# Moving a row norm, its scale factors and a token product in the written order of a two-stream recurrence

## The reference, cut to what matters

```python
gate = ki @ w0_;  hb = ki @ w2_;  sg = silu(gate);  hidden = sg * hb
dhidden = vi @ w1_.transpose(0, 2, 1)
dhbm = dhidden * sg;  dgate = dhidden * hb;  dgba = silu_backprop(dgate, gate)
w1g = newtonschulz5(einsum(hidden * lr1i, vi))      # two steps:
w0g = newtonschulz5(einsum(ki * lr0i, dgba))        #   A = X X^T; Bm = b A + c A A
w2g = newtonschulz5(einsum(ki * lr2i, dhbm))        #   X = a X + Bm X
w1_ = w1_ + w1g                                     # same for w0_, w2_
w1_ = w1_ / (norm(w1_, axis=1) + 1e-05) * w1n       # same for w0_, w2_
oi = silu(qi @ w0_) * (qi @ w2_) @ w1_
```

## Time and profile before

| | |
|---|---|
| time, median of 3 runs | 1683.79 us (1683.41 to 1691.88) |
| span of the profiled execution | 1633.0 us (its own time is not given; the 50.8 us between span and median lie around the instructions) |
| PE busy | 1477.8 us, 90% |
| DVE busy | 1275.3 us, 78% |
| ACT busy | 1004.9 us, 62% |
| POOL busy | 788.0 us, 48% |
| granted PE clock in 300 to 750 us | 1.00 |

### The profile page before, as it was taken

The page is one execution under the profiler, slowest core; times in us unless marked ns, Lnnn a source line. Parts: engine busy times, 40 slices in busy tenths (PEclk is TensorE's granted clock), DMA queues, the critical chain, the costliest instruction groups (busy, mean ns, idle before and its releaser), DMA issues. The chain is left out here.

```text
span 1633.0 us, 44257 instructions
## 1 busy us (share of the span) xinstructions
PE 1477.8 (90%) x12478; PEld 987.5 (60%) x12543; DVE 1275.3 (78%) x4523; ACT 1004.9 (62%) x2284; POOL 788.0 (48%) x837
## 2 busy tenths in 40 slices
PE   7995899999999999999985399999999999999996
PEld 4664677777777777776764255555555555555774
DVE  4663678888888888888886687777777777774998
ACT  4773577666777676777663166666666666663221
POOL 1332234666766666666667434443434443443333
PEclk9996899999999999999997599999999999999998
DMA  3875454445555543223322466766677676633996
GB/s 117 259 234 158 133 155 132 145 135 157 180 164 167 156 144 90 84 85 99 99 69 104 153 189 201 216 201 198 207 201 204 196 210 195 205 89 78 260 259 152
DMA packets 264982, 264.39 MB, mean 162 GB/s; under 512 B 87467, under 2 KB 236313, under 8 KB 264752
## 3 DMA queue, kind: packets, MB, share of 16 engines
q1 hardware_dynamic: 204464, 176.51, 37.4%
q0 software_dynamic: 19968, 51.16, 8.6%
q10 hardware_dynamic: 40320, 33.96, 8.5%
HBM read 142.70 MB, written 122.98 MB: 163 GB/s over the span
## 5 line engine op out<-in xcount | busy, mean ns | idle before, releaser
L1736 POOL DMA_INDIRECT scratch_y<-eo,goes x224 | 225.4, 1006 | 338.6 <-ACT eo L1830 297.1
L1761 PE MATMUL e_psGU<-wexp,e_xT 128*64 x896 | 290.5, 467 | 0.2 <-issue 0.2
L1763 PE MATMUL e_psGU<-e_up,e_xT 128*64 128x352 f32 x896 | 290.5, 467 | 0.0
L1378 POOL TENSOR_TENSOR f_wnr<-f_wss,f_half 128x4 f32<-128x4 f32 x96 | 112.3, 1169 | 197.3 <-DVE f_wss L1201 197.2
L1368 POOL DMA_INDIRECT scratch_buf<-rows,dest x180 | 183.3, 1018 | 44.0 <-issue 44.0
L1851 ACT ACTIVATE e_up<-wexp 128x704 f32 x224 | 177.1, 790 | 20.4 <-POOLq L1726 20.2
L1761 PEld LDWEIGHTS e_psGU<-wexp,e_xT 128*64 128x64 f32 x896 | 113.7, 137 | 122.0 <-issue 122.0
L1971 DVE COPY e_down<-wexp 128x512 f32 x224 | 93.9, 419 | 94.2 <-PE e_psD L1786 92.8
L1830 ACT ACTIVATE eo<-e_psD 128x256 f32<-128x256 f32 x224 | 85.5, 384 | 95.2 <-PE e_psD L1786 47.7
L1819 ACT ACTIVATE e_sgm<-e_psGU 128x176 f32<-128x176 f32 x224 | 71.2, 318 | 77.7 <-PE e_psGU L1763 60.8
L1780 PE MATMUL e_psD<-wexp,e_hT 112*64 x448 | 115.2, 379 | 1.6 <-DVE e_hT L1926 1.6
(11 more groups left out here) (335 smaller groups left out, 4362.1 us busy)
## 6 DMA issues: line engine op xcount, KB each, us to landing
e_xg<-scratch_buf ACTq DMA_DIRECT2D x436, 66.0 KB
scratch_y<-f_blank SPq DMA_DIRECT2D x64, 384.0 KB
c_g<-scratch_y SPq DMA_DIRECT2D x64, 384.0 KB, 9.5
scratch_qkvT<-q_tT SPq DMA_DIRECT2D x16, 768.0 KB, 5.1
wexp<-in_wgT SPq DMA_DIRECT2D x64, 176.0 KB
wexp<-in_wuT SPq DMA_DIRECT2D x64, 176.0 KB
scratch_buf<-f_blank SPq DMA_DIRECT2D x65, 132.0 KB, 1.9
scratch_kv<-q_y SPq DMA_DIRECT2D x16, 512.0 KB, 2.8
```

Of the source, the lines that this page charges most:

```text
L1378: pool.tensor_tensor(wnr[:, x, cols], wss[:, x, cols], half[:, 0:Q], ALU.pow).then_inc(wn1[x].sem, 1)
L1736: pool.indirect_dma_start(out=T["y"], out_offset=bass.IndirectOffsetOnAxis(goes[:, n:n + 1], 0), in_=eo[:, n % OB, :], in_offset=None, bou ...
L1761: pe.matmul(psGU[0:RT, n % 2, 0:2 * F], xT[:, n % 4, k, 0:RT], ring[:, bass.ds(at[n] + k * 2 * F, 2 * F)], start=(k == 0), stop=(k == KD - 1))
L1763: mm = pe.matmul(psGU[RT:P, n % 2, 0:2 * F], xT[:, n % 4, k, RT:P], up2[:, n % 2, k * 2 * F:(k + 1) * 2 * F], start=(k == 0), stop=(k == K ...
```

## The change

The tables of PE and DVE change; ACT, POOL and SyncE keep their order, and no instruction is added or taken away. In each half: `hidden_back` moves on PE from behind `turn_o` to ahead of the first `gram2`; `row_norms` of lot 2 (W1) moves on DVE from between the second and third `b` to behind `pick`; `factors` of lot 2 moves from behind `place` to between the second and third `a`.

```diff
@@ PE_ORDER, first half; the second is the same with the streams exchanged
-    ("x2t", 1, 1, 0), ("x2t", 1, 1, 1), ("hidden_base", 0, 0), ("x2", 1, 1, 1, 1), ("gram2", 1, 1, 0),
+    ("x2t", 1, 1, 0), ("x2t", 1, 1, 1), ("hidden_base", 0, 0), ("x2", 1, 1, 1, 1), ("hidden_back", 0, 0), ("gram2", 1, 1, 0),
...
-    ("gram2", 1, 1, 2), ("turn_o", 0, 2, 1), ("hidden_back", 0, 0), ("poly2", 1, 1, 1), ("poly2", 1, 1, 2),
+    ("gram2", 1, 1, 2), ("turn_o", 0, 2, 1), ("poly2", 1, 1, 1), ("poly2", 1, 1, 2),
@@ DVE_ORDER
-    ("totals", 0, 0), ("update", 1, 1, 2), ("pick", 0, 3), ("factors", 1, 1, 1), ("renorm", 1, 1, 1),
-    ("norm_x", 0, 2), ("norms", 0, 0), ("a", 0, 0, 0), ("a", 0, 0, 1), ("a", 0, 0, 2), ("b", 0, 0, 0),
-    ("b", 0, 0, 1), ("row_norms", 1, 1, 2), ("b", 0, 0, 2), ("read", 0, 1, 0), ("place", 0, 3), ("factors", 1, 1, 2),
+    ("totals", 0, 0), ("update", 1, 1, 2), ("pick", 0, 3), ("row_norms", 1, 1, 2), ("factors", 1, 1, 1), ("renorm", 1, 1, 1),
+    ("norm_x", 0, 2), ("norms", 0, 0), ("a", 0, 0, 0), ("a", 0, 0, 1), ("factors", 1, 1, 2), ("a", 0, 0, 2), ("b", 0, 0, 0),
+    ("b", 0, 0, 1), ("b", 0, 0, 2), ("read", 0, 1, 0), ("place", 0, 3),
```

More of the change, by code:

```diff
@@ L508 @@
 DVE_ORDER = (
-    ("renorm", 0, 1, 1), ("norm_x", 1, 3), ("norms", 1, 1), ("a", 1, 1, 0), ("a", 1, 1, 1), ("a", 1, 1, 2),
-    ("b", 1, 1, 0), ("b", 1, 1, 1), ("row_norms", 0, 1, 2), ("b", 1, 1, 2), ("read", 1, 2, 0), ("place", 1, 4),
-    ("factors", 0, 1, 2), ("gate", 0, 0), ("slope", 0, 0), ("slope_2", 0, 0), ("both", 0, 0), ("token_dg", 0, 0),
+    ("renorm", 0, 1, 1), ("norm_x", 1, 3), ("norms", 1, 1), ("a", 1, 1, 0), ("a", 1, 1, 1), ("factors", 0, 1, 2), ("a", 1, 1, 2),
+    ("b", 1, 1, 0), ("b", 1, 1, 1), ("b", 1, 1, 2), ("read", 1, 2, 0), ("place", 1, 4),
+    ("gate", 0, 0), ("slope", 0, 0), ("slope_2", 0, 0), ("both", 0, 0), ("token_dg", 0, 0),
     ("rows_x", 1, 3), ("token_dhb", 0, 0), ("update", 1, 1, 0), ("token_hid", 0, 0), ("row_norms", 1, 1, 0), ("update", 1, 1, 1), ("squares", 0, 0, 0), ("gate_x", 0, 2, 0), ("squares", 0, 0, 1),
     ("factors", 1, 1, 0), ("squares", 0, 0, 2), ("row_norms", 1, 1, 1), ("row_sums", 0, 0), ("renorm", 1, 1, 0),
-    ("totals", 0, 0), ("update", 1, 1, 2), ("pick", 0, 3), ("factors", 1, 1, 1), ("renorm", 1, 1, 1),
-    ("norm_x", 0, 2), ("norms", 0, 0), ("a", 0, 0, 0), ("a", 0, 0, 1), ("a", 0, 0, 2), ("b", 0, 0, 0),
-    ("b", 0, 0, 1), ("row_norms", 1, 1, 2), ("b", 0, 0, 2), ("read", 0, 1, 0), ("place", 0, 3), ("factors", 1, 1, 2),
+    ("totals", 0, 0), ("update", 1, 1, 2), ("pick", 0, 3), ("row_norms", 1, 1, 2), ("factors", 1, 1, 1), ("renorm", 1, 1, 1),
+    ("norm_x", 0, 2), ("norms", 0, 0), ("a", 0, 0, 0), ("a", 0, 0, 1), ("factors", 1, 1, 2), ("a", 0, 0, 2), ("b", 0, 0, 0),
+    ("b", 0, 0, 1), ("b", 0, 0, 2), ("read", 0, 1, 0), ("place", 0, 3),
     ("gate", 1, 0), ("slope", 1, 0), ("slope_2", 1, 0), ("both", 1, 0), ("token_dg", 1, 0), ("rows_x", 0, 2),
@@ L520 @@
     ("squares", 1, 0, 2), ("row_norms", 0, 0, 1), ("row_sums", 1, 0), ("renorm", 0, 0, 0), ("totals", 1, 0),
-    ("update", 0, 0, 2), ("pick", 1, 3), ("factors", 0, 0, 1),
+    ("update", 0, 0, 2), ("pick", 1, 3), ("row_norms", 0, 0, 2), ("factors", 0, 0, 1),
 )
```

## The result

| | before | changed |
|---|---|---|
| time, median of 4 runs | 1686.85 us (1683.41 to 1691.88) | 1732.07 us (1723.66 to 1738.85) |
| span of the profiled execution | 1633.0 us | 1734.6 us (its own time: 1736.32) |
| PE, DVE busy in the profile | 1477.8, 1275.3 us | 1531.9, 1282.7 us |

The ratio is 1.0266, 95% interval 1.0224 to 1.0307: 45 us slower. The forecast had the direction and 20 us; 1732 lies outside its range of 1684 to 1714.

What follows compares the result with a forecast made beforehand. A loop from DVE to the first Bm, through PE and ACT's Newton-Schulz step, to `last` was taken to set the 22.2 us period. 25 x 0.75 = 18.8 us plus about 1 gave 1683.8 + 20, say 1704 us, range 1684 to 1714.

Steps and rivals of the forecast that it cites:

- The path: Recurrence half: DVE from update to first Bm, PE and ACT through Newton-Schulz, PE to `last`, back to DVE; period 22.2 us.
- the sum: Delays added along one half: third A 1.14 us later, `project` 0.70, second update 0.75; 25 halves give 18.8 us.
- The wait for POOL's root: DVE at the moved W1 factors waits some 0.27 us for POOL's root, bounds 0 and 0.60.
- f_pp does not wait: DVE's 1.26 us wait for `hidden_back` ahead of f_pp goes; DVE then waits for `last` at both updates.
- ACT's and PE's longer waits: ACT's wait for first `x2` about 2.1 us, was 1.73; PE's wait for f_WT about 1.4, was 0.77.
- The rival that set PE first: PE's sum of work sets the period: 0.39 us less a half, 1674 us, or 1669 with 0.58; chance 0.14.
- the 1652 us: Removing DVE's gap ahead of f_pp gains the whole 31.4 us; given little chance.
- The second rival: Root in time, ACT's copy doesn't decide: 0.34 us a half, about 1691 us, called no change; chance 0.16.
- The term from `x2` to `project`: ACT's block moves 0.99 us with `x2`; `project` starts 0.70 later, behind the copy of the third `x2`.
- `hidden_back`'s slot: PE, second Gram matrix: 0.58 us, mostly inside a 0.39 wait for ACT; 0.05 counted as reaching ACT's third A2 copy.
- The early halves: Some seven halves without picks, where the W1 sum fits DVE's idle 1.13 us: about +1 us for all.
- The 50.8 us lie around the instructions: Median of the runs lies 50.8 us above the profiled span; taken as outside it and unchanged by the change.

Runs made afterwards that it cites:

- thinned: Kernel before and changed kernel, each without the gamma and beta matmuls of the second step's polynomials, chip 14: 1623.64 and 1657.53 us.

## Why the prediction was wrong

**The path was right.** With the update of lot 1 at 591.27 - 23.11 = 568.16, the third A comes 11.07 us behind it where it was 9.95: 1.12 later, 1.14 in the sum. `x2` comes 0.99 later, as said (580.62 - 568.16 = 12.46, against 517.70 - 506.23 = 11.47). The wait for POOL's root is 0.23 (578.70 to 578.93), 0.27 in the sum. The root takes 1.01 beside the A's, 1.01 before in its old place. Here the trace agrees with the Trainium skill, page "SBUF — State Buffer", section "🔬 SBUF: two separate sides". f_pp does not wait, the first `gram2` does not wait, and ACT's and PE's longer waits are there (2.13, 1.36). The rival that set PE first is out. DVE's gap at f_pp went and the time rose, so the 1652 us is out too that the forecast worked out for that gap with the page "Perfetto Trace Analysis" of the Trainium skill, section "Optimization Strategy". (The second rival's sum gives 1692 us, not the 1691 written; nothing hangs on it.)

**The term from `x2` to `project` was too small.** I had 0.70 from the copy, and 0.75 in all. The copy of the third `x2` comes 7.35 us behind the first `x2`, 7.23 before: `hidden_back`'s slot reaches ACT's third A2 copy (4.90 to 5.05) and through it this one with 0.12, where I took 0.05 of the bounds 0 and 0.2. Behind the copy `project` starts after 0.75 us, 0.92 before: PE had 0.17 to give, not the 0.29 that I took by letting it start 0.04 behind the copy's end; it starts 0.14 behind it. 0.99 + 0.12 - 0.17 - 0.03 (`project` to `last`, 2.12 against 2.15) = 0.91 a half, 22.8 us in all in place of 18.8.

**No term stood for the granted clock, nor for what lies behind the recurrence.** This is the step that failed: the sum took 25 equal halves, all at clock 1.00 as before, and put the other stages at 0 because their instructions stay the same. On chip 8 the change costs 38 us where the sum has 20, and only 4 of the missing 18 are mis-sized terms of the path. The ledger of two pairs of profiles, in us of span; the first pair is the earlier trace rows's profile and chip 8, the second chip 11 and the profile after. Neither pair is known to be from one chip, so the second above all, whose kernels before differ by some 8 us (1686.85 and 1694 to 1696), is rough:

| | before | changed | more | before | changed | more |
|---|---|---|---|---|---|---|
| to the recurrence | 154.4 | 154.7 | 0.3 | 152.9 | 153.6 | 0.7 |
| 6 early halves | 125.8 | 125.7 | -0.1 | 125.0 | 125.2 | 0.2 |
| 25 halves | 555.0 | 587.0 | 32.0 | 601.8 | 636.0 | 34.2 |
| the rest | 797.8 | 802.3 | 4.5 | 814.6 | 819.8 | 5.2 |
| span | 1633.0 | 1669.7 | 36.7 | 1694.2 | 1734.6 | 40.4 |

Of the 32.0, 22.8 are the longer period, 8.0 the five halves of low clock (24.72 against 23.11), and 1.0 the first of the 25, which takes 24.13 us. Of the 34.2, 25 x (24.33 - 23.59) = 18.5 are the period, and the other 15.7 that twelve halves in place of four fall below clock 1.00, 2.3 and 3.0 us longer on the mean than those at full clock. The early halves cost nothing in the sum, where I had 1 us. In the first pair that is a balance, not rest: the first of the six is 2.3 us shorter and the other five are 2.2 longer. The 4.5 and 5.2 behind the recurrence I had put at 0; in the first pair the clock of the 25 us behind it is 0.93 in place of 1.00, and of what else they are made I don't know. That the low clock itself follows from the change isn't shown in its cause: each changed kernel's profile has more low halves than the profile of its kind without the change (5 against 0, 12 against 4, thinned 2 against 1), and nothing that was tried took them away.

**The base was read wrongly.** "The 50.8 us lie around the instructions" was an assertion without a row. It was a difference between two executions, by all that was measured later between two kinds of chip. Even without it the forecast fails: the change costs 38 us on one kind and 45 to 49 on the other. But it hid that where the kernel before takes 1683 us and more its halves are nearer 23.6 us (chip 11) than 22.2, that `last` is taken up there 2.0 to 4.0 us behind its recorded start, with DVE idle up to 2.3 us for it, and that stretches of low clock are there already.

**What stays open.** Why on some chips the signals of dense matmuls come late at a granted clock of 1.00; what makes the clock fall; why moving the sum costs 37 us and adding one 19; whether filling the wait at `back` would remove the low halves on a chip of the 1633 us kind. Of the kernels that compute the whole reference none beats the kernel before.

## What to carry to other kernels

When a profile's span and the timed runs differ by more than a few microseconds, ask for a profile whose own time is near the median before pricing anything: prices read from another execution miss waits that the timed one has. What was added to the critical path was paid here at more than its length (19 us for 15, 38 to 49 for 23). On chip 8 about half of the surplus, 8 of 16 us, lies in halves in which the clock fell. Many of those begin at a longer wait of PE, but not all, and the same wait mostly stands without them (1.36 us in 20 of 25 halves on chip 8, 23 of 25 on chip 14). So put a range for the clock beside the sum, not a rule. And a wait that costs nothing is a margin: moving 1.39 us of work into 1.26 us of it cost 7 to 8 us on both chips, and delaying the product that f_pp waits for made that wait 3.9 us (chip 11).

## What the runs showed of the hardware

The same program takes 1632 to 1634 us on chips 14 and 8 and 1683 to 1696 on 11, 15, 0 and 3, though the profiles of both kinds report a granted clock of 1.00 in most of the recurrence. On the latter the consumer of a matmul in a dense stretch is released up to 4.0 us behind its recorded start (`last` in the kernel before, chip 11), where 0.43 is usual. The delay comes in steps: there it is 2.04 to 2.05, 2.73 to 2.77 or 3.4 to 4.0 us in all but two of the 25 halves. Several signals then arrive together, 0.06 to 0.12 us apart, though 0.6 and 1.1 us of work lie between them. A record's end says there when the instruction should have been done; only the start on the next engine says when it was handed over.

The granted clock fell to 1.2 GHz right behind idle times of PE of 1.36 to 2.1 us, but on chip 8 also 9 us behind the last idle time over 0.25 us, and the same idle time of 1.36 us mostly had no fall behind it.
